# Two pairs of groups, half the stages apart, in a four-layer graph network's layer loop

## The reference

```
L0  relu((U^T x) W1 + b1) W2 + b2, times U       U: eigenvectors of the normalized Laplacian
L1  two graph convolutions: h = relu(adj (x Wg + bg)); then for p = 1..4 an LSTM over each
    window of p neighbouring nodes (Wih[p-1], Whh[p-1]); its last state replaces the
    window's last node
L2  graph attention: Wh = h W; softmax over masked leaky(s1 + s2); times Wh
L3  four-head attention with head size 32: softmax(q k^T / sqrt(32) + mask) v
```

## Time and profile before

| | |
|---|---|
| median of 3 runs | 1653.32 us (1651.76 to 1654.76) |
| profiled execution | 1649.82 us |
| its span, first to last instruction | 1648.1 us |
| TensorE, VectorE, ScalarE, GpSimd busy | 1091.9, 1224.9, 886.5, 175.3 us |
| mean granted TensorE clock | 0.888 |

### The profile page before, as it was taken

One profiled execution on the slowest core, in us unless ns is written; L12 is line 12 of the kernel. 1 busy time (PEld: TensorE's weight loads), 2 busy tenths in 40 slices (PEclk: granted clock), 3 DMA queues, 4 the chain that ended last, 5 costly groups with the idle time before them and its releaser, 6 DMA issues.

```text
span 1648.1 us, 28261 instructions
## 1 busy us (share of the span) xinstructions
PE 1091.9 (66%) x6196; PEld 895.7 (54%) x6196; DVE 1224.9 (74%) x5776; ACT 886.5 (54%) x3054; POOL 175.3 (11%) x316
## 2 busy tenths in 40 slices
PE   5666666666666200000199887998879988799885
PEld 4555555555555100000068766688666886669764
DVE  6888888888888899999645668556695566855677
ACT  4555555555555100000057777676776767767786
POOL 1111111111111000000011110111101111111111
PEclk9999999999999955555599988998899989899897
DMA  0000000000000300000000000100001000000000
GB/s 2 0 0 0 0 0 0 0 0 0 0 0 0 68 1 1 1 1 1 26 26 1 1 1 14 41 1 1 1 14 41 1 1 1 14 14 1 1 1 26
DMA packets 19858, 12.49 MB, mean 8 GB/s; under 512 B 1153, under 2 KB 18722, under 8 KB 19746
## 3 DMA queue, kind: packets, MB, share of 16 engines
q1 hardware_dynamic: 19746, 11.23, 2.5%
HBM read 7.03 MB, written 4.19 MB: 7 GB/s over the span
## 4 chain that ended last, share of the span: by engine, by line
PE 30%; DVE 10%; ACT 7%; issue 2%; POOL 1%; DMA 0%; DVEq 0%; POOLq 0%; ACTq 0%
PE P L933 10%; PE P L878 6%; PE P L941 5%; PE P L883 2%; ACT x L1036 2%; ACT S L1110 2%; DVE S L1224 1%; PE P L966 1%; PE P L996 1%; DVE top L1229 1%; DVE stats L1149 1%; DVE t L1242 1%; PE P L950 1%; PE P L962 1%; PE P L980 1%
## 5 line engine op out<-in xcount | busy, mean ns | idle before, releaser
L164 PE MATMUL tailP<-tail_ident 128*128 128x129 f32 x254 | 101.5, 502 | 133.0 <-DVE tail_ident L280 132.1
L164 PEld LDWEIGHTS tailP<-tail_ident 128*128 128x128 f32 x254 | 63.5, 311 | 170.4 <-DVE tail_ident L280 169.2
L386 PE MATMUL sumP<-tail_ident,Yb 128*128 128x128 f32 x1 | 0.5, 473 | 215.0 <-DVE Yb L525 215.0
L188 ACT ACTIVATE small<-tailP,tiny 128x1 f32<-128x1 f32 x127 | 33.3, 262 | 192.3 <-PE tailP L164 192.3
L174 PE MATMUL zP<-QT,w_col 128*128 128x128 f32 x254 | 101.1, 501 | 40.2 <-ACT w_col L196 40.2
L395 ACT ACTIVATE small<-small 128x1 f32<-128x1 f32 x1 | 0.2, 202 | 235.5 <-DVE small L501 235.5
L933 PE MATMUL P<-t,WihT 128*128 128x128 f32 (+1 forms) x832 | 119.4, 290 | 9.7 <-POOL t L866 9.7
L941 PE MATMUL P<-step_h,WhhT 128*128 128x128 f32 (+2 forms) x768 | 123.4, 304 | 0.0
L386 PEld LDWEIGHTS sumP<-tail_ident,Yb 128*128 128x128 f32 x1 | 0.2, 183 | 215.1 <-DVE Yb L525 215.1
L933 PEld LDWEIGHTS P<-t,WihT 128*128 128x128 f32 x832 | 109.9, 191 | 13.2 <-POOL t L866 12.5
L1059 ACT ACTIVATE gate_i<-P,half_bias 128x128 f32<-128x128 f32 (+3 forms) x160 | 69.1, 432 | 88.1 <-PE P L941 65.3
(11 more groups left out here) (289 smaller groups left out, 3367.5 us busy)
## 6 DMA issues: line engine op xcount, KB each, us to landing
xin<-x SPq DMA_DIRECT2D x16, 256.0 KB, 2.9
out<-y SPq DMA_DIRECT2D x16, 256.0 KB, 2.3
W<-L_gnn_W SPq DMA_DIRECT2D x3, 64.0 KB
Wqkv<-L_gnn_W SPq DMA_DIRECT2D x1, 192.0 KB
Wg<-L_gnn_Wg SPq DMA_DIRECT2D x2, 64.0 KB
A<-adj SPq DMA_DIRECT2D x1, 64.0 KB, 1.8
b<-L_gnn_b SPq DMA_DIRECT2D x1, 64.0 KB
bg<-L_gnn_bg SPq DMA_DIRECT2D x1, 64.0 KB
```

The costliest lines, as they stand in the source:

```text
L164: pe.matmul(tailP[:, 0:1 + N], tails, tail_ident[:], start=True, stop=True).then_inc(tail_row_ready, 1)
```

## The change

Slots 0 and 1 stay a place apart, and so do slots 2 and 3, but the second pair follows the first by 24 places, and `head` has 27 places. While slots 0 and 1 are in stage k, slots 2 and 3 are 24 stages behind, or 31 ahead in the trip before. Since slots no longer come by in turn, each semaphore that is signalled several times a trip (`REPEATED`) becomes two, one for each pair, and waits count within the pair. Instructions, tiles and banks are the same. Line numbers rise by 10 from `layers` on.

```diff
-SKEW = 1
-HEAD_STAGES = 4
+TWIN = 2
+LAG = (0, 1, 24, 25)
+HEAD_STAGES = 27
...
-    def S_(name):
-        if name not in named:
-            named[name] = sem(name)
-        return named[name]
+    def S_(name, s=None):
+        label = name if name not in REPEATED else f"{name}_{s // TWIN}"
+        if label not in named:
+            named[label] = sem(label)
+        return named[label]
...
-    place = {(name, s): k + SKEW * s for k, name in enumerate(stages) for s in range(SLOTS)}
+    place = {(name, s): k + LAG[s] for k, name in enumerate(stages) for s in range(SLOTS)}
...
     def rank(occurrences, k, s):
 
-        return [entry for entry in order if entry[0] in occurrences].index((occurrences[k], s)) + 1
+        return [entry for entry in order if entry[0] in occurrences and entry[1] // TWIN == s // TWIN].index(
+            (occurrences[k], s)) + 1
...
         def at(name, occurrences, k, s, trip):
-            engine.wait_ge(S_(name), trip * (len(occurrences) * SLOTS) + rank(occurrences, k, s))
+            engine.wait_ge(S_(name, s), trip * (len(occurrences) * TWIN) + rank(occurrences, k, s))
```

More of the change, by code:

```diff
@@ L936, in stage @@
                         if gate == G_ and not t:
-                            last.then_inc(S_("gates_ig_ready"), 1)
+                            last.then_inc(S_("gates_ig_ready", s), 1)
                     if t:
@@ L943, in stage @@
                             if gate == G_:
-                                last.then_inc(S_("gates_ig_ready"), 1)
+                                last.then_inc(S_("gates_ig_ready", s), 1)
                     if p > 1:
-                        last.then_inc(S_("gates_fo_ready"), 1)
+                        last.then_inc(S_("gates_fo_ready", s), 1)
                 elif name[0] == "output":
@@ L997, in stage @@
                                              kT[s][at:at + HEAD, b, :], start=True, stop=True, tile_position=(at, 0))
-                    last.then_inc(S_("scores_ready"), 1)
+                    last.then_inc(S_("scores_ready", s), 1)
                 elif name[0] == "probs_turned":
                     on_pair("probs_ready", name[1], s, trip)
-                    turn(P[s][0], lambda b: S[s][:, 0, b, :]).then_inc(S_("probs_turned_a"), 1)
-                    turn(P[s][1], lambda b: S[s][:, 1, b, :]).then_inc(S_("probs_turned_b"), 1)
+                    turn(P[s][0], lambda b: S[s][:, 0, b, :]).then_inc(S_("probs_turned_a", s), 1)
+                    turn(P[s][1], lambda b: S[s][:, 1, b, :]).then_inc(S_("probs_turned_b", s), 1)
                 elif name[0] == "mixed":
@@ L1011, in stage @@
                                              ST[s][:, h, b, :], start=True, stop=True, tile_position=(0, at))
-                    last.then_inc(S_("mixed_ready"), 1)
+                    last.then_inc(S_("mixed_ready", s), 1)
                 elif name == "heads_turned":
@@ L1074, in stage @@
                     on_step("cell_ready", p, t, s, trip)
[L1075 removed]
+                    A_.activation(gg[s][:, 0:m], cell[s][:, 0:m], ACT.Tanh, scale=0.5).then_inc(S_("cell_tanh_ready", s), 1)
                 elif name == "turn_2":
@@ L1111, in stage @@
                                                  accum_out=total[s][:, k:k + 1])
-                    last.then_inc(S_("probs_ready"), 1)
+                    last.then_inc(S_("probs_ready", s), 1)
                 elif name[0] == "probs_turned":
@@ L1124, in signal @@
             def signal(instruction, name, s):
-                instruction.then_inc(S_(name), 1)
+                instruction.then_inc(S_(name, s), 1)
             for s in range(SLOTS):
```

22 lines of the change are left out of this document (13 added, 9 removed).

## The result

The changed kernel is slower: median 1735.34 us (1731.61 to 1739.82, four runs) against 1654.04 us for the kernel before, a ratio of 1.0487 (95% interval 1.0459 to 1.0515). The forecast was 1630 us, and its range ended at 1680. The profiled execution took 1739.82 us around a span of 1738.1.

What follows compares the result with a forecast made beforehand. One stage was taken as bound by TensorE, the other by chains over three engines. Ramps 124 plus mixed places 681 gave 805 us against 828.4, 23 less: median 1630 us, eight-in-ten range 1585 to 1680.

Steps and rivals of the forecast that it cites:

- 85% of it TensorE's work: Trips with both pairs under way: 191 us each was forecast, with TensorE's work as 85% of that.
- the most to win: Layers: TensorE's work of 162 us a trip was taken as the floor under 207, leaving 45 us a trip.
- The mixed places: The 196 steps of the order with both pairs under way, forecast at 191 us per 55 steps, 681 us in all.
- place sum: Largest engine's work at each step of the order, added over a trip: 190.5 us in the old pairing, 200.8 in the new.
- the walked cycles: Four-step cycles in the attention rounds, traced through the engines' lists: 15.5 and 16.5 us, 0.90 of their summed largest-engine work.
- Ramps: Start and end of the layers with one pair alone: head 56 us plus tail 68 us, together 124 us.
- rival 3: Stretches with one pair alone run at half clock: 14 us more, 1644 us; chances 0.06 (gain eaten to within 3.3 us), 0.04 (past it).
- two groups alone keep TensorE full: Head's recurrent steps: two groups bring 3.6 us of TensorE work against a 3.3 us chain, losing only about 8 us.
- Rival 1: Engines' lumps of work lend freely between neighbouring steps: 172.6 us a trip, 89 us less, 1564 us; chance 0.14.
- Rival 2: Exponentials block the recurrence's tanhs in ScalarE's list and steps can't lend: 218 us a trip, 1727 us; chance 0.18.
- mixed trips of over 198: Sign for wrong, in trips with both pairs under way, together with TensorE idling 3 us before recurrent matmuls; 186 to 196 meant right.
- a tail of over 80: Sign for wrong: the last 25 steps, second pair alone, take over 80 us; some 65 to 75 meant right.

Runs made afterwards that it cites:

- the pair's own run: Kernel with two slots only (LAG 0, 1), eight trips of two groups, all work done; 2105.58 us in all, 160 us a trip.
- the orders within a place: Groups listed from slot 3 to 0 at each step of the order: old lag 1712.84 us, ratio 1.0342; lag 24 1772.12 us, 1.0676, both against the kernel before.
- the two edits tried: Changed kernel with the recurrent pair first in every list (1748.2 us), or with one 0.15 us VectorE copy first in its place (1742.61 us).
- the one with the copy ahead: Changed kernel with the 0.15 us copy s1 (stage edges) first in its place in VectorE's list alone; 1742.61 us, ratio 1.0553 against the kernel before.
- the four other lags: Second pair 24, 25, 27 or 12 places behind the first, against the old lag of 1: 1735.3, 1738.4, 1787.8 and 1751.3 us.

## Why the prediction was wrong

**What bounds the kernel.** That an old trip is bound mostly by TensorE held: leaving 27 us of its work out gave 15 to 17. The premise that carried the gain, "85% of it TensorE's work" in a mixed trip, was near the share for which TensorE is busy (181.9 of 210.6 us) and wrong as a bound: there 27 us of its work are worth 6.7. Counting 45 us as "the most to win" was sound arithmetic on a floor that neither order comes near.

**The mixed places: the failed step.** It is the 191 us for a trip, which is 0.95 of the place sum of 200.8; measured are 211.5, 1.05 of it. The 191 had two parts. Where a pair is in the rounds (the first pair's stages 10 to 23 and 44 to 54) neighbouring places were to lend, at the 0.90 of the walked cycles; elsewhere the place sum stood nearly as it was, with nothing for waits above it. By the first pair's stage:

| stages | place sum us | forecast us | measured us |
|---|---|---|---|
| 0 to 9 | 30.3 | 31 | 30.6 |
| 10 to 23 | 58.6 | 53 | 59.1 |
| 24 to 34 | 34.0 | 34 | 36.5 |
| 35 to 43 | 35.2 | 34 | 43.1 |
| 44 to 54 | 42.7 | 39 | 41.3 |
| trip | 200.8 | 191 | 210.6 |

In the two stretches with lending 8.4 of the 19.6 us are missed. The walk itself was too short: between starts of a group's scores the trace has 16.6 us (1190.76 to 1207.35) for a walked 15.5, and with the second pair in the rounds 17.0 and 17.8 (1065.85 to 1082.86, 1069.63 to 1087.46) for a walked 16.5. That is 0.97 and 0.93 to 0.98 of the place sums, so there is a little lending in the rounds, and none over the stretches that have them beside norms and turns. The other 11.2 us, most of them in stages 35 to 43, are waits above the place sum, which I had put at next to nothing though the old order showed 1.087. There one pair has norms, turns and the edge softmax, and the other its first steps with 512 and 256 columns. I take it that long single latencies of both pairs stand in turn in the same lists there, as in the chain above; no run isolates it. My own table had the warning: the new sum is 10 us above the old one. Only the lending took the forecast under the 197.6 us at which nothing is won, and it was tested against two neighbouring stages of four groups.

**The old trip.** 207 was 204.8 in steady state, which took 2 of my 16 us of gain away.

**Ramps.** The second failed step. Forecast 124, measured 152: first ten stages 26.5 against 21, recurrent stages 45 against 27 + 8, tail 80.5 against 68. The mechanism, a pair alone is a chain, was right; the sizes were not. One reading was wrong too: the 7.0 us for "two groups' work" in stages 0 to 9 is one group's (three matmuls of 512 columns and 20 of 128); two have 14.1, of which 13.2 fall into the first ten places, and TensorE is busy there for 20.8 us, at a clock of 0.68. The error isn't in the sum, which took that stretch as a chain. The clock of rows with four groups (0.85 and 0.82) was carried to stretches with two, which get 0.68 and 0.64: rival 3 had priced that at 5 us in the first ten stages, which would be 26, and at 9 in the tail, which would be 77, and so found half of the 28 us. And "two groups alone keep TensorE full" was wrong: the window of the head has it busy for 34.1 of 45.0 us, and in the pair's own run a last step of period 4 takes both groups 4.33 us (1214.86 to 1219.19 between starts of L951), not 3.6.

**The rivals.** Rival 1, free lending, is far off. Rival 2 gave 1727 us, 8 from the median, and by its sum (trip 218, ramps 124) it had one term too large and one too small, so that it came so near is luck. Tanhs do wait longer (54.8 us for 13.5), but that the eight exponentials in front of them are what holds the trip is refuted, for with one in place of eight the trip is still 208. Its other half, that places don't lend, fits the trips at 1.05 to 1.10 of their sums; but with 20 us taken off the sum the trip only fell by 10, so the sum is a floor and not what holds it. Rival 3, half clock in the ramps, was right in place and size, as far as it went, but 14 us alone would still have left a gain.

**What would show it.** Of the signs named, "mixed trips of over 198" and "a tail of over 80" came true, but so did two signs for right, nearly: TensorE's slices at 8 or 9, and the new wait for the cell tanh. They don't tell a fast trip from a slow one. "TensorE idle 3 us at a time before its recurrent matmuls" did only in front of the periods' first ones, for the window copies (4.6 us at the longest). No table loads between tanh and exponential appeared: pricing them at nothing was right. The changed layers have a single load, at 856.7, where there were three.

**What stays open.** The runs with work left out and the orders within a place show that no engine's sum of work sets the new order's trip; that chains across groups do is argued from this and from one stretch of the trace. Which handovers make up the 20 us by which the forecast missed isn't settled: of the two edits tried, the one with the copy ahead moved the wait, and neither shortened the trip. Nor was a lag found that beats 1; by the place sum none of the 24,804 ways to give three slots a lag within a trip is below the old order's 190.5 (a calculation, with nothing measured in it), and the four other lags that ran on the chip agree with that as far as they go. None of the kernels with all the work beats the one before by more than its measurement can tell.

## What to carry to other kernels

Before two phases are overlapped, measure one group alone and one pair alone: here 143 and 160 us, against 205 for four, which says at once that four neighbouring groups already overlap well and that the ramps of a pair will cost nearly its whole chain, at the clock that it gets alone. The largest engine's work, summed place by place, was a floor under every whole trip here; a lag that raises it (200.8 for 190.5) starts with a loss, and a "lending" factor walked came out too low even where it was walked. Price the handovers above that sum with the ratio that the kernel already shows. To ask whether an engine bounds a stretch, take some of its work out and see how much comes back per us (some 0.6 before, 0.25 after), rather than reading its busy share, and look at the clock of both runs, since it can fall when work goes.

## What the runs showed of the hardware

The part before the layers has the same code in all kernels, and its length varied between profiles: the layers start at 818.7 us in the run with lag 27, at 819.7 before, 830.2 in the changed kernel and 845.2 in the run with lag 24 and one exponential. So 10.5 of the 90 us between the profiled executions of the two kernels have nothing to do with the change, and the layers' own span was the better measure. What makes that part vary I didn't find out. And a mean granted clock of 0.60 was seen in the window of a group alone, where TensorE's matmuls are busy for 77.4 of 143.3 us: that is close to its lower level of 1.2 GHz for most of the time, though the engine was never idle for more than 6.07 us at a stretch in that trip's rows.
